# Graph layer with residual norm: every fifth bank of edge counts copied out of PSUM by VectorE

## The chip, the cores and the metric

One NeuronCore of a Trainium2 chip runs the whole kernel. The metric is the device time of one execution in microseconds (us), as the median of several runs. TensorE multiplies matrices into PSUM, VectorE and ScalarE work on vectors and can read PSUM, GpSimd and SyncE serve DMAs here.

## The reference

The graph has N = 6250 nodes of D = 128 features and E = 206250 edges, sorted by their destination:

```
msg = x[src] + edge_attr
agg = segment_sum(msg, dst, N)
h = relu(agg @ W1 + b1) @ W2 + b2
h = (h - mean(h)) * rsqrt(var(h) + 1e-5) * ln_w + ln_b
h = graph_norm(h)
out = layernorm(x + gelu(h) + x)
```

The change touches only how the sums of `x[src]` over the edges of a node are made.

## The kernel before

**Sums of x as a product with counts.** Row `x[src]` is never fetched. The kernel takes 25 chunks of 250 destination nodes. For a chunk it makes `counts[p, q, n]`, how many edges go from source node 128q + p to node n, and then multiplies: 49 tiles q, each as a high and a low part of x (`x_hi`, `x_lo`), so 98 matmuls of 128x250 that add up in one PSUM bank (`count_chunk`, L689 to L695).

**Counts as products of marks.** The 250 nodes of a chunk are 125 pairs. For each pair up to 128 edges lie in 128 partitions, and VectorE writes two tables of ones and zeros, of the source's low seven bits and of its tile and place in the pair (`mark_batch`, L971 to L984, two instructions at L982 for 25 pairs; five batches in a chunk). One matmul of the two tables gives the counts of one pair, 98 columns of PSUM (L672). Five pairs fill a bank of 490 columns, so a chunk has 25 banks, numbered k = 0 to 24. They go round a ring of three PSUM banks (`cps`, `RING = 3`), and ScalarE copies each into `counts` (`copy_chunk`, L514 to L526). TensorE waits for ScalarE's copy of bank k - 3 before it writes bank k (L669), and for all 25 before the 98 matmuls (L689).

**Between the banks.** After banks 2, 8, 14 and 20 TensorE sums half a group of `edge_attr` rows (`sum_half`, L622, a burst of 12 fp32 matmuls that the trace counts as 24) and after the first and third of these turns the sums of the last group (`turn_sums`, L636). After bank 20 it waits for VectorE's keys of the next chunk and turns them (`turn_keys`, L653 to L657), and ScalarE copies the turned keys (`copy_keys`, L495) before its copies of banks 21 to 24.

**VectorE's order** is written by hand. While TensorE does the 98 matmuls, `head` makes batches 0 to 2 of the chunk's marks (slots for three batches, so batch 3 must wait until batch 0 is used up, that is until bank 4 is done). Then `rest` (L1016 to L1028) adds the finished sums (`add_chunk`, L1034), finds rows for the next chunk (`stage_row`), makes batch 3, marks and adds for the edge groups (`mark` L875, `add` L892, `put` L880), makes batch 4, and at last `make_keys` (L949 to L969), a chain of nine short instructions on rows that GpSimd gathered. The next chunk's `head` begins with `stage_tile` (L935).

Ahead of the 25 chunks lies a stage for the index lists and the first edge groups, behind them the two dense layers and the norms. The change leaves both alone.

Of the kernel before, what the change touches and what calls it, by code (L numbers as in the profile page):

```python
# [39 lines left out]
PAIR = 2  # L40
# [4 lines left out]
BATCHES = PAIRS // BATCH  # L45
# [4 lines left out]
BANK = 5  # L50
BANKS = PAIRS // BANK
BPB = BATCH // BANK
CREDIT = BPB + 1
RING = 3
SHIFT = 7
DST_SHIFT = 13
NO_EDGE = (1 << 30) - 1
# [13 lines left out]
def gnn_kernel(nc, x, src, dst, edge_attr, W1, b1, W2, b2, ln_w, ln_b, gn_w, gn_b, gn_ms, out):  # L71
# [37 lines left out]
    with ExitStack() as ctx:  # L109
# [6 lines left out]
        def sem(name):  # L116
            return ctx.enter_context(nc.semaphore(name))
# [97 lines left out]
        eps = [b[:, 0:D] for b in banks[3:5]]  # L215
        turned_sum = [b[:, D:D + SPREAD] for b in banks[3:5]]
        turn_ps, sps = banks[6], banks[7]
        KEY0, LO0 = 0, P
        zps = [banks[u][:, :].rearrange("p (k n) -> p k n", k=HC) for u in range(2)]
        hps = [banks[2], banks[3]]  # L220
# [42 lines left out]
        marks_ready = sem("marks_ready")  # L263
        banks_done = sem("banks_done")
        banks_free = sem("banks_free")
        chunk_summed = sem("chunk_summed")
        chunk_added = sem("chunk_added")
        cover_in = sem("cover_in")
# [49 lines left out]
        g_rest = edge_attr[g_rest0:g_rest0 + G_REST_P * G_TILES, :].rearrange("(p j) d -> p (j d)", j=G_TILES)  # L318
        g_last = edge_attr[g_rest0 + G_REST_P * G_TILES:E, :].rearrange("(a j) d -> a (j d)", a=1)
        dst_tiles = dst[0:ET * SPAN].rearrange("(t e) -> t e", e=SPAN)  # L320

        def column(a):
            return a.rearrange("(p a) -> p a", a=1)
# [78 lines left out]
        @block.gpsimd  # L402
        def _(pool):
            pool.iota(iota_i[:, :], [[1, P]], base=0, channel_multiplier=0)
            pool.iota(prow_i[:, :], [[0, 1]], base=0, channel_multiplier=1)
            pool.iota(pair_i[:, :], [[PAIR * PAIRS, CHUNKS + 1]], base=0, channel_multiplier=PAIR)
            pool.memset(ones_b[:, :], 1.0)
            pool.memset(ones[:, :], 1.0).then_inc(consts_ready, 1)
            half = SEARCH * PAIRS
            for at, to in ((0, half), (half, NPAIR + 7)):  # L410
                pool.iota(pair_row[:, at:to], [[1, to - at]], base=at, channel_multiplier=0,
                          allow_small_or_imprecise_dtypes=True).then_inc(pair_row_ready, 1)
            for s, places in ((halves_free, HALVES), (sums_copied, 3), (sums_turned, 3), (edges_added, 2),
                              (banks_done, CREDIT), (chunk_summed, 1), (chunk_added, 1)):
                pool.sem_inc(s, places)
            pool.wait_ge(turned, TURNS)
            pool.wait_ge(listed_stored, 64)
            pool.memset(agg[:, :], 0.0).then_inc(agg_zeroed, 1)
            pool.wait_ge(below_ready, 2 * SETS)
            pool.iota(listing[:, 0:P * INTER], [[1, P], [0, INTER]], base=0, channel_multiplier=0,  # L420
                      allow_small_or_imprecise_dtypes=True).then_inc(pads_ready, 1)


            with pool.Fori(0, CHUNKS + 1) as c:
                pool.wait_ge(listed_stored, 64)
                pool.wait_ge(tile_staged, c + 1)
                pool.sem_inc(gathers_begun, 1)
                for k in range(2):
                    pool.indirect_dma_start(begins[0:PAIRS, k * P:(k + 1) * P], None, listed_rows,  # L429
                                            bass.IndirectOffsetOnAxis(tile_slot[0:PAIRS, k:k + 1], 0)  # L430
                                            ).then_inc(begins_loaded, 16)
                pool.wait_ge(row_staged, c + 1)
                pool.sem_inc(gathers_begun, 1)
                pool.indirect_dma_start(near[0:PAIRS, :], None, listed_rows,  # L434
                                        bass.IndirectOffsetOnAxis(row_slot[0:PAIRS, 0:1], 0)
                                        ).then_inc(near_loaded, 16)


            pool.wait_ge(mode_ready, 1)
            with pool.If(pool.value_load(flag_i[0:1, 0:1], min_val=0, max_val=1) > 0):  # L440
                with pool.Fori(0, PASSES * G_GROUPS) as n:
                    pool.wait_ge(group_loaded, (n + 1) * 128)
                    pool.sem_inc(gathers_begun, 1)
                    for j in range(G_TILES):
                        pool.indirect_dma_start(g_edges[:, 2 + j // G_HALF, (j % G_HALF) * D:(j % G_HALF + 1) * D], None, x,
                                                bass.IndirectOffsetOnAxis(edge_src[:, j:j + 1], 0)
                                                ).then_inc(group_gathered, 16)

        @block.scalar
        def _(act):  # L450
# [63 lines left out]
            def copy_chunk(c):  # L514
                act.wait_ge(chunk_summed, c + 1)
                for k in range(BANKS):
                    act.wait_ge(banks_done, c * BANKS + (k + 1 + CREDIT))
                    nodes = BANK * PAIR
                    nc.scalar.copy(counts[:, :, k * nodes:(k + 1) * nodes].rearrange("p q (i m) -> p q i m", m=PAIR),  # L519
                                   cps[k % RING][:, 0:nodes * NT].rearrange("p (i q m) -> p q i m", q=NT, m=PAIR)  # L520
                                   ).then_inc(banks_free, 1)
                    if k in SUMS_AT:
                        j = SUMS_AT.index(k)
                        copy_sums(c * GPC + (LEAD * GPC + j), j)
                    if k == KEYS_AT:
                        copy_keys(c + 1)  # L526
# [61 lines left out]
        def _(pe):  # L588
# [74 lines left out]
            def count_chunk(c):  # L663
                for k in range(BANKS):
                    b = k // BPB
                    if k % BPB == 0:
                        pe.wait_ge(marks_ready, c * BATCHES + (b + 1))
                    if k >= RING:
                        pe.wait_ge(banks_free, c * BANKS + (k + 1 - RING))  # L669
                    for i in range(BANK):  # L670
                        n = (k % BPB) * BANK + i
                        last = nc.tensor.matmul(cps[k % RING][:, i * KEYS:(i + 1) * KEYS],  # L672
                                                mark_lo[b % MARKED][:, n // INTER, :, n % INTER],
                                                mark_key[b % MARKED][:, n // INTER, :, n % INTER],
                                                start=(i == 0), stop=(i == BANK - 1),
                                                skip_group_check=True)
                    last.then_inc(banks_done, 1)
                    if k in BURSTS:
                        u = BURSTS.index(k)
                        g = c * GPC + (LEAD * GPC + u // 2)  # L680
                        begin_half(g, u % 2, edge_loaded[u], (c + LEAD) * 16 + 16)
                        sum_half(u, u // 2, u % 2)
                        if u % 2 == 0:
                            turn_sums(g - 1, (u // 2 - 1) % GPC)
                    if k == KEYS_AT:
                        pe.wait_ge(keys_ready, c * 2 + 2)
                        turn_keys(c + 1)

                pe.wait_ge(banks_free, (c + 1) * BANKS)  # L689
                pe.wait_ge(chunk_added, c + 1)  # L690
                for q in range(NT):
                    for part in (x_hi, x_lo):
                        last = nc.tensor.matmul(sps[:, 0:CHUNK], part[:, q, :], counts[:, q, :],  # L693
                                                start=(q == 0 and part is x_hi), stop=(q == NT - 1 and part is x_lo))
                last.then_inc(chunk_summed, 1)  # L695
# [95 lines left out]
        def _(dve):  # L791
# [142 lines left out]
            def stage_tile(c):  # L934
                dve.tensor_copy(tile_slot[0:PAIRS, :], tile_rows[0:PAIRS, bass.ds(c, 1), :].rearrange(  # L935
                    "p a k -> p (a k)")).then_inc(tile_staged, 1)
# [34 lines left out]
            def mark_batch(c, b):  # L971
# [11 lines left out]
                                             of.to_broadcast([P, BLOCKS_B, n, INTER]), ALU.is_equal)  # L983
                last.then_inc(marks_ready, 1)  # L984

            stage_tile(0)
            with dve.Fori(2, LEAD - 3) as r:
                round_groups(r)
# [27 lines left out]
            def rest(c, before, groups):  # L1016
                g = c * GPC + LEAD * GPC
                base = base_of(g + (1 - GPC))
                if before is not None:
                    add_chunk(before, groups)  # L1020
                stage_row(c + 1)
                mark_batch(c, 3)
                mark(g + 1, 0, 1)
                add(g + (1 - GPC), 1, base, c + 1)
                mark(g + 1, 1, 1)
                put(g + 1, 1)
                mark_batch(c, 4)
                make_keys(c + 1)  # L1028

            def add_chunk(c, groups):  # L1030
                dve.wait_ge(chunk_summed, c + 2)
# [220 lines left out]
```

## Time and profile before

| | us |
|---|---|
| median of three runs | 906.94 (905.07 to 907.28) |
| the profiled execution | 911.31 |
| its span, first to last instruction | 909.3 |
| VectorE busy (share of the span) | 678.4 (75%) |
| ScalarE busy | 383.4 (42%) |
| ScalarE copies of counts, 625 | 318.3 |
| TensorE, 2450 matmuls with the counts | 584.1 busy |

TensorE's busy time is that of modelled ends, which overlap; starts are exact. A row of the timeline merges instructions of one line that follow one another. The number in brackets is idle time of the engine ahead of the row, and behind the arrow stands what ended it. In the table of stretches, PEclk is the granted clock: 1.00 is 2.4 GHz and 0.50 is 1.2 GHz.

### The profile page before, as it was taken

To read this page: it belongs to the slowest core of one execution; us is meant where nothing else is said; L and a number is where in the kernel's file an instruction comes from. 1 tells how busy PE (TensorE), PEld (TensorE's weight loads), DVE (VectorE), ACT (ScalarE), POOL (GpSimd) and SP (SyncE) were. 2 spreads that over 40 slices of the span, in tenths; PEclk is the share of its full clock that TensorE was granted. 3 is DMA by queue.
4 is the path that set the end of the run, shared out by engine and by line. 5 is a ranking of instruction groups with operands and counts; after the bars stand their busy time and mean duration, and the time that the engine had idled before them with its cause. 6 is when DMAs were issued, how large, how long until landed. Compare 5 with 4: busy or idle time off the path is not lost.

```text
span 909.3 us, 25887 instructions
## 1 busy us (share of the span) xinstructions
PE 729.4 (80%) x9449; PEld 633.5 (70%) x9449; DVE 678.4 (75%) x1185; ACT 383.4 (42%) x841; POOL 145.4 (16%) x91
## 2 busy tenths in 40 slices
PE   3486569888988888988889988889988889989950
PEld 2464448777877777877777877777877777877830
DVE  5844777877878877878877878877878877844576
ACT  0200034355433555433554433554434554424464
POOL 1210022120221220221120221220221220200000
PEclk9987989899999999999999999999999999999975
DMA  6669973443334443334444334443334444303004
GB/s 173 228 216 361 360 262 99 124 147 115 104 100 121 147 144 116 106 97 125 147 144 114 107 94 128 147 144 112 109 93 130 147 144 113 94 25 141 0 1 141
DMA packets 89477, 123.25 MB, mean 136 GB/s; under 512 B 9029, under 2 KB 85018, under 8 KB 89260
## 3 DMA queue, kind: packets, MB, share of 16 engines
q1 hardware_dynamic: 78992, 112.83, 39.9%
q0 software_dynamic: 6240, 5.08, 2.1%
q10 hardware_dynamic: 4228, 5.12, 1.8%
q8 instruction: 10, 0.16, 0.1%
q14 instruction: 7, 0.05, 0.0%
HBM read 118.91 MB, written 4.03 MB: 135 GB/s over the span
## 4 chain that ended last, share of the span: by engine, by line
PE 48%; DVE 26%; issue 11%; DMA 7%; ACT 5%; DVEq 2%; ACTq 1%; POOL 0%; SPq 0%; POOLq 0%
PE bank L693 33%; DVE pool_m L982 12%; DMA edges<-in_edge_attr_dram 5%; PE bank L622 3%; PE bank L672 3%; ACT counts L519 3%; DVE onehot L875 3%; PE bank L740 3%; PE bank L750 2%; PE bank L656 1%; PE bank L636 1%; DMA agg<-in_dst_dram 1%; DMA begins<-listed,tile_slot 1%; DVE node_f L965 1%; DVE node_f L957 1%
## 5 line engine op out<-in xcount | busy, mean ns | idle before, releaser
L519 ACT CAST counts<-bank 128x490 fp32r<-128x490 f32 x625 | 318.3, 606 | 324.0 <-PE bank L672 324.0
L693 PE MATMUL bank<-counts,x_hi 128*128 128x250 f32 x1225 | 293.5, 284 | 29.6 <-ACT counts L519 29.6
L693 PE MATMUL bank<-counts,x_lo 128*128 128x250 f32 x1225 | 290.6, 281 | 0.0
L982 DVE TENSOR_TENSOR pool_m<-listing,turned_lo 128x3328 bf16<-128x3328 bf16 x125 | 236.7, 1893 | 30.1 <-PE bank L672 26.7
L693 PEld LDWEIGHTS bank<-counts,x_hi 128*128 128x128 f32 x1225 | 234.8, 192 | 33.4 <-ACT counts L519 33.4
L672 PE MATMUL bank<-pool_m 128*128 128x98 bf16 x3125 | 211.2, 210 | 33.0 <-ACT counts L519 22.7
L693 PEld LDWEIGHTS bank<-counts,x_lo 128*128 128x128 f32 x1225 | 235.2, 192 | 0.0
L672 PEld LDWEIGHTS bank<-pool_m 128*128 128x128 bf16 x3125 | 161.9, 99 | 77.6 <-ACT counts L519 75.2
L982 DVE TENSOR_TENSOR pool_m<-listing,turned_key 128x2548 bf16<-128x2548 bf16 x125 | 184.5, 1476 | 0.0
L622 PE MATMUL bank<-edges,onehot 128*32 128x128 f32 x3228 | 126.7, 293 | 30.1 <-DMA edges<-in_edge_attr_dram 23.3
L429 POOL DMA_INDIRECT begins<-listed,tile_slot x52 | 101.9, 1959 | 297.1 <-DVE tile_slot L935 265.2
L622 PEld LDWEIGHTS bank<-edges,onehot 128*32 128x32 f32 x3228 | 88.8, 116 | 46.7 <-issue 20.7
L434 POOL DMA_INDIRECT begins<-listed,row_slot x26 | 33.0, 1270 | 310.6 <-DVE row_slot L946 298.4
L875 DVE TENSOR_TENSOR onehot<-iota_f,dst_cols 128x384 f32<-128x384 f32 x136 | 74.5, 550 | 1.1 <-PE bank L622 0.9
L1034 DVE TENSOR_TENSOR agg<-agg,bank 128x250 f32 (+1 forms) x25 | 10.4, 416 | 75.4 <-PE bank L693 74.6
L489 ACT COPY sums<-bank 128x128 f32<-128x128 f32 x68 | 20.2, 297 | 85.0 <-PE bank L622 85.0
L892 DVE TENSOR_TENSOR agg<-agg,bank 128x128 f32 x68 | 19.0, 280 | 39.4 <-PE bank L636 38.3
L595 PE MATMUL bank<-ones_b,pool_m 128*125 128x1 bf16 x175 | 19.2, 245 | 23.1 <-DVE pool_m L826 23.1
L595 PEld LDWEIGHTS bank<-ones_b,pool_m 128*125 128x125 bf16 x175 | 19.0, 229 | 23.3 <-DVE pool_m L826 23.3
L636 PE MATMUL bank<-place,sums 128*128 128x128 f32 x136 | 34.7, 339 | 0.4 <-ACT sums L489 0.4
L636 PEld LDWEIGHTS bank<-place,sums 128*128 128x128 f32 x136 | 21.2, 197 | 14.9 <-issue 14.0
L546 ACT ACTIVATE onehot<-bank,b1c 128x250 f32<-128x250 f32 x50 | 20.7, 466 | 25.3 <-PE bank L740 25.3
(149 smaller groups left out, 407.9 us busy)
## 6 DMA issues: line engine op xcount, KB each, us to landing
edges<-in_edge_attr_dram SPq DMA_DIRECT2D x134, 768.0 KB, 4.5
out_dram<-pool_m SPq DMA_DIRECT2D x6, 512.0 KB
begins<-listed,tile_slot POOLq DMA_INDIRECT x52, 4.2
agg<-in_dst_dram SPq DMA_DIRECT2D x1, 768.0 KB
agg<-in_src_dram ACTq DMA_DIRECT2D x1, 768.0 KB
listed<-agg ACTq DMA_DIRECT2D x1, 768.0 KB
begins<-listed,row_slot POOLq DMA_INDIRECT x26, 4.3
w<-in_L_gnn_W_dram ACTq DMA_DIRECT2D x2, 128.0 KB, 2.2
```

What stands on the lines that cost most here:

```text
L429: pool.indirect_dma_start(begins[0:PAIRS, k * P:(k + 1) * P], None, listed_rows, bass.IndirectOffsetOnAxis(tile_slot[0:PAIRS, k:k + 1], 0) ...
L434: pool.indirect_dma_start(near[0:PAIRS, :], None, listed_rows, bass.IndirectOffsetOnAxis(row_slot[0:PAIRS, 0:1], 0)).then_inc(near_loaded, 16)
L519: nc.scalar.copy(counts[:, :, k * nodes:(k + 1) * nodes].rearrange("p q (i m) -> p q i m", m=PAIR), cps[k % RING][:, 0:nodes * NT].rearran ...
L546: nc.scalar.activation(hidden[:, u, c, :], zps[u][:, c, 0:CHUNK], ACT.Relu, bias=b1c[:, c:c + 1]).then_inc(hidden_ready, 1)
L595: last = nc.tensor.matmul(turn_ps[0:PAIRS, c:c + 1], below[:, i % BELOW, at:at + PAIRS], ones_b[:, :], start=(c == 0 and i == 0), stop=(i ...
L622: last = nc.tensor.matmul(eps[s][b * WINDOW:(b + 1) * WINDOW, :], oh[:, t, :], edges[:, u, t * D:(t + 1) * D], start=(k == 0 and j == 0), ...
L636: nc.tensor.matmul(turned_sum[s], sums[:, :], place[:, s, :], start=True, stop=True).then_inc(sums_turned, 1)
L672: last = nc.tensor.matmul(cps[k % RING][:, i * KEYS:(i + 1) * KEYS], mark_lo[b % MARKED][:, n // INTER, :, n % INTER], mark_key[b % MARKED ...
L693: last = nc.tensor.matmul(sps[:, 0:CHUNK], part[:, q, :], counts[:, q, :], start=(q == 0 and part is x_hi), stop=(q == NT - 1 and part is ...
L740: last = nc.tensor.matmul(zps[u][:, k, 0:CHUNK], w1[:, k * P:(k + 1) * P], agg[:, bass.ds(c * CHUNK, CHUNK)], start=True, stop=True, skip_ ...
L875: dve.tensor_tensor(oh, window, of.to_broadcast([P, HALF, WINDOW]), ALU.is_equal).then_inc(onehot_ready, 1)
L982: last = dve.tensor_tensor(to[b % MARKED], values[:, :, 0:n, :].to_broadcast([P, BLOCKS_B, n, INTER]), of.to_broadcast([P, BLOCKS_B, n, IN ...
```

## The change

The last bank of each batch (k = 4, 9, 14, 19 and 24) now goes into a PSUM bank of its own (`own_ps`, the unused `banks[5]`), and VectorE copies it (`copy_bank`). The other 20 banks of a chunk keep the ring of three and ScalarE. A new semaphore `own_free` tells TensorE that the bank of its own has been copied. In `rest` the five copies stand between the other steps, and batch 4 moves ahead of `add`, the second `mark` and `put`. The core of the diff:

```diff
+SHARED = BPB - 1
+        own_ps = banks[5]
+        own_free = sem("own_free")
...
 def copy_chunk(c):
     act.wait_ge(chunk_summed, c + 1)
     for k in range(BANKS):
-        act.wait_ge(banks_done, c * BANKS + (k + 1 + CREDIT))
-        nodes = BANK * PAIR
-        nc.scalar.copy(counts[:, :, k * nodes:(k + 1) * nodes].rearrange("p q (i m) -> p q i m", m=PAIR),
-                       cps[k % RING][:, 0:nodes * NT].rearrange("p (i q m) -> p q i m", q=NT, m=PAIR)
-                       ).then_inc(banks_free, 1)
+        if k % BPB < SHARED:
+            act.wait_ge(banks_done, c * BANKS + (k + 1 + CREDIT))
+            nc.scalar.copy(bank_counts(k), in_order(cps[(k - k // BPB) % RING])).then_inc(banks_free, 1)
...
 def count_chunk(c):
-        if k >= RING:
-            pe.wait_ge(banks_free, c * BANKS + (k + 1 - RING))
+        own, turn = k % BPB == SHARED, k - b
+        to = own_ps if own else cps[turn % RING]
+        if own:
+            pe.wait_ge(own_free, c * BATCHES + (b + 1))
+        elif turn >= RING:
+            pe.wait_ge(banks_free, c * (BATCHES * SHARED) + (turn + 1 - RING))
...
-    pe.wait_ge(banks_free, (c + 1) * BANKS)
+    pe.wait_ge(banks_free, (c + 1) * (BATCHES * SHARED))
+    pe.wait_ge(own_free, (c + 1) * BATCHES + 1)
...
+def copy_bank(c, b):
+    dve.wait_ge(banks_done, c * BANKS + ((b + 1) * BPB + CREDIT))
+    dve.tensor_copy(bank_counts(b * BPB + SHARED), in_order(own_ps)).then_inc(own_free, 1)
...
 def rest(c, before, groups):
     stage_row(c + 1)
+    copy_bank(c, 0)
     mark_batch(c, 3)
     mark(g + 1, 0, 1)
+    copy_bank(c, 1)
+    mark_batch(c, 4)
     add(g + (1 - GPC), 1, base, c + 1)
     mark(g + 1, 1, 1)
     put(g + 1, 1)
-    mark_batch(c, 4)
+    copy_bank(c, 2)
     make_keys(c + 1)
+    copy_bank(c, 3)
+    copy_bank(c, 4)
```

The change moves instructions on VectorE and TensorE. First, VectorE in `rest`, from the end of `stage_row` on. Before (`pool_m` holds the marks, `onehot` those of the edge groups):

```order
L946 TENSOR_SCALAR row_slot<-first_i 125x1 [waits prep]
L978 REGISTER_ALU
L982 TENSOR_TENSOR pool_m<-listing,turned_lo 128x3328 [waits banks_done]
L982 TENSOR_TENSOR pool_m<-listing,turned_key 128x2548
L872 ISA
L875 ISA [waits halves_free]
L875 TENSOR_TENSOR onehot<-iota_f,dst_cols 128x384
L887 REGISTER_ALU
L892 ISA [waits chunk_added,edges_added,sums_turned]
L892 TENSOR_TENSOR agg<-agg,bank 128x128
L872 REGISTER_ALU
L875 ISA [waits halves_free]
```

and now, where the row `counts<-bank` is a copy of a bank (49 tiles by 10 nodes):

```order
L959 TENSOR_SCALAR row_slot<-first_i 125x1 [waits prep]
L1000 REGISTER_ALU
L1001 CAST counts<-bank 128x49x10 [waits banks_done]
L995 TENSOR_TENSOR pool_m<-listing,turned_lo 128x3328 [waits banks_done]
L995 TENSOR_TENSOR pool_m<-listing,turned_key 128x2548
L885 ISA
L888 ISA [waits halves_free]
L888 TENSOR_TENSOR onehot<-iota_f,dst_cols 128x384
L1000 REGISTER_ALU
L1001 CAST counts<-bank 128x49x10 [waits banks_done]
L995 TENSOR_TENSOR pool_m<-listing,turned_lo 128x3328 [waits banks_done]
L995 TENSOR_TENSOR pool_m<-listing,turned_key 128x2548
```

The copy of bank 4 stands ahead of batch 3 and the copy of bank 9 ahead of batch 4; the addition to `agg` is gone from between the two batches.

Second, VectorE up to the start of `make_keys` (`lo_i`, `hi_i`, `junk`). Before:

```order
L875 TENSOR_TENSOR onehot<-iota_f,dst_cols 128x384
L880 ISA [waits sums_turned]
L880 TENSOR_SCALAR place<-iota_f,place_row 128x128
L978 REGISTER_ALU
L982 TENSOR_TENSOR pool_m<-listing,turned_lo 128x3328 [waits banks_done]
L982 TENSOR_TENSOR pool_m<-listing,turned_key 128x2548
L950 ISA
L953 TENSOR_SCALAR lo_i<-begins 125x128 [waits near_loaded]
L954 TENSOR_SCALAR hi_i<-begins 125x128
L956 TENSOR_SCALAR junk<-begins 125x128
```

and now:

```order
L888 TENSOR_TENSOR onehot<-iota_f,dst_cols 128x384
L893 ISA [waits sums_turned]
L893 TENSOR_SCALAR place<-iota_f,place_row 128x128
L1000 REGISTER_ALU
L1001 CAST counts<-bank 128x49x10 [waits banks_done]
L963 ISA
L966 TENSOR_SCALAR lo_i<-begins 125x128 [waits near_loaded]
L967 TENSOR_SCALAR hi_i<-begins 125x128
L969 TENSOR_SCALAR junk<-begins 125x128
L943 REGISTER_ALU
L970 REGISTER_ALU [waits prep]
```

Batch 4 no longer stands right ahead of the keys; the copy of bank 14 does. The copies of banks 19 and 24 come behind the keys.

Third, TensorE at the end of a chunk's counts, banks 23 and 24, with the numbers of the PSUM banks. Before:

```order
L669 REGISTER_ALU
L672 MATMUL bank2<-pool_m 128x98 [waits banks_free]
L672 MATMUL bank2<-pool_m 128x98 x4
L669 REGISTER_ALU
L672 MATMUL bank0<-pool_m 128x98 [waits banks_free]
L672 MATMUL bank0<-pool_m 128x98 x4
L689 ISA
L693 MATMUL bank7<-counts,x_hi 128x250 [waits chunk_added,banks_free]
```

and now:

```order
L681 REGISTER_ALU
L684 MATMUL bank1<-pool_m 128x98 [waits banks_free]
L684 MATMUL bank1<-pool_m 128x98 x4
L684 MATMUL bank5<-pool_m 128x98 [waits own_free]
L684 MATMUL bank5<-pool_m 128x98 x4
L701 ISA
L702 ISA [waits banks_free]
L706 MATMUL bank7<-counts,x_hi 128x250 [waits chunk_added,own_free]
```

Bank 24 goes to PSUM bank 5 and waits for VectorE's copy of bank 19; the first of the 98 matmuls waits for ScalarE's copies and for VectorE's.

## Rows read from the trace of the kernel before

**Rows 1.** The page's first part: busy us, share of the span, instructions.

```profile
PE 729.4 (80%) x9449; PEld 633.5 (70%) x9449; DVE 678.4 (75%) x1185; ACT 383.4 (42%) x841; POOL 145.4 (16%) x91
```

**Rows 2.** Timeline of VectorE, addition of each chunk's sums (start us, us, instruction, idle before).

```profile
154.48 0.42 DVE L1034 TENSOR_TENSOR agg<-agg,bank 128x250 f32 x1 [2.90 <-PE bank L693]
...
184.57 0.42 DVE L1034 TENSOR_TENSOR agg<-agg,bank 128x250 f32 x1 [5.72 <-PE bank L693]
...
213.38 0.42 DVE L1034 TENSOR_TENSOR agg<-agg,bank 128x250 f32 x1 [4.43 <-PE bank L693]
...
240.70 0.41 DVE L1034 TENSOR_TENSOR agg<-agg,bank 128x250 f32 x1 [2.94 <-PE bank L693]
...
786.87 0.42 DVE L1034 TENSOR_TENSOR agg<-agg,bank 128x250 f32 x1 [2.90 <-PE bank L693]
```

**Rows 3.** Timeline of TensorE, one steady chunk, from its first bank to its sums.

```profile
404.18 0.87 PE L672 MATMUL bank<-pool_m 128*128 128x98 bf16 x15
...
404.98 0.86 PE L622 MATMUL bank<-edges,onehot 128*32 128x128 f32 x24
...
406.10 0.87 PE L672 MATMUL bank<-pool_m 128*128 128x98 bf16 x15
...
415.09 0.86 PE L622 MATMUL bank<-edges,onehot 128*32 128x128 f32 x24
...
416.92 0.33 PE L656 MATMUL bank<-ident,lo_f 125*128 125x125 f32 x1 [0.97 <-DVE junk L967]
...
417.19 0.86 PE L672 MATMUL bank<-pool_m 128*128 128x98 bf16 x15
...
419.95 0.39 PE L693 MATMUL bank<-counts,x_hi 128*128 128x250 f32 x1 [1.19 <-ACT counts L519]
```

**Rows 4.** Timeline of VectorE in the same chunk, from batch 3 to the next chunk.

```profile
406.76 1.93 DVE L982 TENSOR_TENSOR pool_m<-listing,turned_lo 128x3328 bf16<-128x3328 bf16 x1 [0.89 <-PE bank L672]
...
410.02 0.54 DVE L875 TENSOR_TENSOR onehot<-iota_f,dst_cols 128x384 f32<-128x384 f32 x1
...
414.55 0.21 DVE L953 TENSOR_SCALAR lo_i<-begins 125x128 int32<-125x128 int32 x1
...
416.57 0.28 DVE L967 TENSOR_SCALAR_CACHE_REDUCE junk<-junk 125x128 f32<-125x128 f32 x1
...
416.78 0.08 DVE L967 DVE_READ_ACCUMULATOR junk<-junk  x1
...
417.43 0.17 DVE L935 COPY tile_slot<-tile_rows 125x2 int32 x1 [0.56 <-DVE junk L967]
```

**Rows 5.** Timeline of ScalarE, the end of the same chunk.

```profile
417.39 0.27 ACT L499 CAST turned_lo<-bank 128x125 bf16<-128x125 f32 x1 [1.27 <-PE bank L656]
...
417.70 1.55 ACT L519 CAST counts<-bank 128x490 fp32r<-128x490 f32 x3
...
419.25 0.66 ACT L519 CAST counts<-bank 128x490 fp32r<-128x490 f32 x1
```

**Rows 6.** Timeline of VectorE late in the kernel, and one group by form.

```profile
878.45 0.67 DVE L1174 SCALAR_TENSOR_TENSOR pool_m<-pool_m,bank 128x512 f32 x1
...
879.03 1.64 DVE L1179 BATCH_NORM_STATS2 pool_m<-pool_m  x8
...
L862 DVE CAST dst_cols<-bank 128x408 bf16<-128x408 f32 x4 | 7.6, 2197 | 0.0
```

**Rows 7.** Stretches of TensorE: from:to us, length, PE busy (count), PEclk, DMA share, GB/s.

```profile
164.90:169.20 4.30, 2.47 (x50) 0.99 0.80 258
169.20:176.00 6.80, 6.16 (x29) 0.50 0.19 61
195.60:199.90 4.30, 1.86 (x35) 1.00 0.78 255
199.90:203.30 3.40, 3.38 (x16) 0.50 0.09 28
415.00:419.30 4.30, 2.48 (x50) 1.00 0.78 258
```

More of the change, by code:

```diff
@@ L320, in gnn_kernel, with bank_counts, in_order @@
         dst_tiles = dst[0:ET * SPAN].rearrange("(t e) -> t e", e=SPAN)
+        def bank_counts(k):
+            nodes = BANK * PAIR
+            return counts[:, :, k * nodes:(k + 1) * nodes].rearrange("p q (i m) -> p q i m", m=PAIR)
+        def in_order(bank):
+            return bank[:, 0:BANK * KEYS].rearrange("p (i q m) -> p q i m", q=NT, m=PAIR)
         def column(a):
@@ L413, in _ @@
             for s, places in ((halves_free, HALVES), (sums_copied, 3), (sums_turned, 3), (edges_added, 2),
-                              (banks_done, CREDIT), (chunk_summed, 1), (chunk_added, 1)):
+                              (banks_done, CREDIT), (chunk_summed, 1), (chunk_added, 1), (own_free, 1)):
                 pool.sem_inc(s, places)
@@ L667, in count_chunk @@
                         pe.wait_ge(marks_ready, c * BATCHES + (b + 1))
-                    if k >= RING:
-                        pe.wait_ge(banks_free, c * BANKS + (k + 1 - RING))
+                    own, turn = k % BPB == SHARED, k - b
[4 more added lines that the diff above has]
+                        pe.wait_ge(banks_free, c * (BATCHES * SHARED) + (turn + 1 - RING))
                     for i in range(BANK):
                         n = (k % BPB) * BANK + i
-                        last = nc.tensor.matmul(cps[k % RING][:, i * KEYS:(i + 1) * KEYS],
+                        last = nc.tensor.matmul(to[:, i * KEYS:(i + 1) * KEYS],
                                                 mark_lo[b % MARKED][:, n // INTER, :, n % INTER],
```

## The prediction

> **What bounds the kernel now.** The page's first part comes first: TensorE is busy 80% of the span, VectorE 75%, ScalarE 42% [rows 1]. No engine is full, so the order of waits inside a chunk has to be read. The timeline of VectorE gives the length of a chunk from one addition of sums to the next: (786.87 - 240.70) / 20 = 27.31 us in the steady part [rows 2]. The timeline of TensorE parts such a chunk in two: 25 banks of counts from 404.18 to 419.95, that is 15.77 us, and the 98 matmuls, the other 11.54 us [rows 3]. The matmuls follow one another without a gap, so the change can only act in the 15.77 us.
>
> The reader should see there that TensorE doesn't set the pace. It writes three banks in 0.80 us (404.18 to 404.98), a bank in 0.27, and it sits idle for 0.97 us before it turns the keys at 416.92 and for 1.19 us before the matmuls at 419.95 [rows 3]. The first wait ends with VectorE, the second with ScalarE. VectorE's timeline shows why the first is there: it waits 0.89 us for bank 4, starts batch 3 at 406.76, and from there works without a pause to the end of the keys at 416.78 + 0.08 = 416.86 [rows 4]. **This chain of 10.1 us on VectorE, not the copies on ScalarE, sets when the counts can end.** From the keys to the matmuls it is ScalarE: the turned keys from 417.39, banks 21 to 23 from 417.70 to 419.25, then bank 24 until 419.91 [rows 5], 0.04 us before the first matmul.
>
> **The price of a copy on VectorE.** No copy of this shape is in the trace. The nearest row is the addition late in the kernel that reads 512 columns of fp32 from PSUM: 0.67 us long, and the next instruction starts 0.58 us after it [rows 6]. For 490 columns I take 0.58 x 490 / 512 = 0.56 us of VectorE's time, with its end 0.65 us after its start. A lower bound is half of it, 0.28, if a copy with one source ran at twice the rate. An upper bound is the conversion of `dst_cols`, also out of PSUM: 2197 ns for 408 elements [rows 6], 5.4 ns each, so 2.6 us for 490. That row writes single two-byte values 48 bytes apart; the new copies write ten neighbouring words at a time, so I stay with 0.56.
> The Trainium skill (Vector Engine (DVE) Microarchitecture Reference, section Measured stream behaviour on trn2) states full rate for runs of at least two adjacent words, which the copies have on both sides; by it the upper bound falls away. No row here shows it for this shape.
>
> **Part by part, in a steady chunk.**
> - Removed from ScalarE: five copies. Four of them end nothing that is late. Taking away that of bank 24 lets ScalarE end with bank 23 at 419.25 in place of 419.91: 0.66 us gained at the end of the chain [rows 5].
> - Added to VectorE ahead of the keys: the copies of banks 4, 9 and 14. The first can't use the 0.89 us wait, since it waits for the same bank 4 as batch 3 behind it. All three lie in the unbroken chain: 3 x 0.56 = 1.68 us. Keys at 418.54 in place of 416.86.
> - Batch 4 ahead of the addition, the second mark and the `place`: the same instructions in another order, nothing for the keys.
> - Added behind the keys: the copies of banks 19 and 24. Bank 24 is written 4 x 0.27 = 1.07 us after the turn at 417.19, so at 418.26; with a 0.13 us hand-over and 0.65 us its copy ends at 419.04 on the old clock, before ScalarE's 419.25. Hidden, by 0.2 us.
> - VectorE's next chunk: `stage_tile`, at 417.43 before [rows 4], must now wait for the copy of bank 24, and starts about 3.8 us later, the tables some 3.4 us later (0.36 us of the old gap was a wait for the keys). The matmuls start 1.02 us later. VectorE's wait for them was 2.94 us [rows 2], so about 0.5 us of cover is left. If it were gone, batch 3 would be late next.
> - TensorE's new waits: bank 14 needs the copy of bank 9, which starts at 406.76 + 0.56 + 3.26 + 0.54 = 411.1 and ends at 411.8. After it come a burst and a turn (404.98 to 406.10, 1.12 us) and banks 15 to 18, until about 414.2. Bank 19 needs the copy of bank 14, which starts at 414.55 + 1.12 = 415.7 and ends at 416.3 [rows 3, 4]. Behind that wait stand bank 20 and a burst, 1.3 us, done by 417.7; the keys come at 418.5. Hidden behind the keys, but TensorE is now empty for about 2.1 us at one place and 0.9 at another.
>
> Sum without the clock: 1.68 - 0.66 = 1.02 us a chunk, 25.5 us for 25 chunks.
>
> **The clock.** In two chunks of the kernel before, the granted clock fell to 0.50 at the end of the counts: from 169.2 to 176.0 and from 199.9 to 203.3 [rows 7]. These chunks took 184.57 - 154.48 = 30.09 and 213.38 - 184.57 = 28.81 us, 2.78 and 1.50 more than the steady 27.31 [rows 2]. In the 4.3 us ahead of the falls TensorE was busy 2.47 and 1.86 us; in the steady chunk the stretch like the first has 2.48 and the clock stays up [rows 7]. So the kernel before stands close to the edge. The change makes the stretch emptier: in the 4.3 us from 414.2 to the keys at 418.5 TensorE has 1.3 us of work. I therefore expect a fall in nearly every chunk. Its price is between 1.50 and 2.78, mean 2.14; I add 0.2, since the turn of the keys (0.27 us), now at the lower clock as well, lies on the path: 2.3 us. For 24 chunks, the first one left out, 55.2 us.
> The Trainium skill (TensorE: Matmul & The Clock Gate, section HAM oscillation) puts the danger in single long gaps of TensorE; by that rule the gaps here would be too short and the term nothing, 932.4 us in all. The falls of the two chunks came with gaps of about 1 us, as the steady chunk's 0.97 and 1.19 [rows 3], so the trace speaks against it.
>
> **The forecast.** The profiled execution took 911.31 us, 4.37 above the median of 906.94. The two falls in it (2.78 + 1.50 = 4.28) explain nearly all of that, and I put every chunk's clock into its own term: 911.31 - 4.28 + 25.5 + 55.2 = 987.7, so **988 us**.
>
> **The rivals.**
> - *The clock stays up*, or falls as seldom as before: for it, the steady chunk, which has such gaps and keeps it; against it, the emptier stretch. 906.94 + 25.5 = 932.4 us. If it falls in half of the chunks, 932.4 + 12 x 2.3 = 960.
> - *The copies come cheap and the end of the chain is what counts* (faster): ScalarE's last copy ends 0.66 us earlier in each chunk, and the copies on VectorE find room in its waits. Then 906.94 - 25 x 0.66 = 890.4 us. It decides where the three copies together cost less than 0.66 us, 0.22 each, in the chain. Against it: even the lower bound of 0.28 is above that, and there is no pause in the chain [rows 4]. At that lower bound the chunk loses 0.84 - 0.66 = 0.18 us, 911 us without falls.
> - *The copies are slow because of their strides*: with 2.6 us each the keys come 7.8 us later, 7.1 us a chunk, and the time passes 1080.
> - *The change does not do what it says*, in that ScalarE stays the last in a chunk: that is so in my sum too, and there its gain is only the 0.66.
>
> **How the numbers follow.** A measurement here tells 0.3% from no change. Falls in nearly every chunk: 0.62, from 907 + 25.5 + 24 x 1.50 = 968.5 to 907 + 25.5 + 24 x (2.78 + 0.2) = 1004. Falls in about half: 0.12. None or few: 0.17. Slower copies, over 1005: 0.03. These are slower, 0.94. Break-even near 0.22 us a copy: 0.03 for no change. The cheap copies: 0.03 for faster. The range goes from 930, which takes in the case without falls, to 1005.
>
> **What would show it.** On VectorE's timeline, three copies of about 0.65 us between batch 3 and the keys, and keys some 1.7 us later after bank 4. On TensorE's, a wait of about 2 us ahead of bank 19 that ends with VectorE, and a chunk length near 30.6 us (28.3 without falls). In the stretches, a granted clock of 0.50 at the start of the 98 matmuls in most chunks. The forecast is wrong if the copies start to end in well under 0.3 us, if VectorE waits between batch 3 and the keys, or if the clock reads 1.00 throughout.

## The result: 991.15 us, 1.0924 times the time before

| | before | after |
|---|---|---|
| median of four runs each, us | 907.11 (905.07 to 909.91) | 991.15 (989.94 to 992.18) |
| ratio, 95% interval | | 1.0924 (1.089 to 1.0957) |
| the profiled execution, its span | 911.31, 909.3 | 989.94, 987.9 |

The kernel lost 84.0 us; 988 was predicted. The size and the sign came out, but the trace shows that two steps of the working did not happen as told. The profile page of the kernel after has this in its first part, its line of the granted clock, and its row for the new copies (busy us, mean ns, idle time before them):

```profile
PE 756.1 (77%) x9449; PEld 671.8 (68%) x9449; DVE 751.3 (76%) x1310; ACT 328.4 (33%) x716; POOL 139.9 (14%) x91
...
PEclk9976778988889888899888998889988899889975
...
L1001 DVE CAST counts<-bank 128x490 fp32r<-128x490 f32 x125 | 83.0, 664 | 95.2 <-PE bank L684 95.2
```

Against [rows 1] VectorE gained 125 instructions and 73 us of busy time, ScalarE lost 55. The clock is down all along the 25 chunks, not in two of them.

VectorE's timeline of the kernel after, additions of two chunks (start us, us, instruction, idle before):

```profile
525.30 0.42 DVE L1056 TENSOR_TENSOR agg<-agg,bank 128x250 f32 x1 [1.31 <-PE bank L706]
...
556.02 0.41 DVE L1056 TENSOR_TENSOR agg<-agg,bank 128x250 f32 x1 [1.30 <-PE bank L706]
```

A chunk takes 556.02 - 525.30 = 30.72 us, where it took 27.31 [rows 2]: 3.41 more. VectorE's wait for the matmuls shrank from 2.90 to 1.31 and did not vanish. Between those rows, VectorE's timeline of the same chunk:

```profile
527.48 0.67 DVE L1001 CAST counts<-bank 128x490 fp32r<-128x490 f32 x1 [0.89 <-PE bank L684]
528.06 1.88 DVE L995 TENSOR_TENSOR pool_m<-listing,turned_lo 128x3328 bf16<-128x3328 bf16 x1
...
531.73 0.66 DVE L1001 CAST counts<-bank 128x490 fp32r<-128x490 f32 x1
532.30 1.88 DVE L995 TENSOR_TENSOR pool_m<-listing,turned_lo 128x3328 bf16<-128x3328 bf16 x1
...
535.50 0.28 DVE L905 TENSOR_TENSOR agg<-agg,bank 128x128 f32 x1
...
536.36 0.66 DVE L1001 CAST counts<-bank 128x490 fp32r<-128x490 f32 x1
536.94 0.21 DVE L966 TENSOR_SCALAR lo_i<-begins 125x128 int32<-125x128 int32 x1
...
539.17 0.08 DVE L980 DVE_READ_ACCUMULATOR junk<-junk  x1
540.17 0.67 DVE L1001 CAST counts<-bank 128x490 fp32r<-128x490 f32 x1 [0.92 <-PE bank L684]
542.94 0.67 DVE L1001 CAST counts<-bank 128x490 fp32r<-128x490 f32 x1 [2.10 <-PE bank L684]
```

The copy is 0.66 us long and the next instruction starts 0.57 or 0.58 after it. From bank 4 to the keys VectorE still works without a pause: 527.48 to 539.25 is 11.77 us, 1.67 more than the 10.10 of [rows 4]. But the keys are not what TensorE waits for. Its timeline in the same chunk:

```profile
524.89 0.87 PE L684 MATMUL bank<-pool_m 128*128 128x98 bf16 x15
...
532.44 0.40 PE L684 MATMUL bank<-pool_m 128*128 128x98 bf16 x5 [1.25 <-DVE counts L1001]
535.83 1.51 PE L630 MATMUL bank<-edges,onehot 128*32 128x128 f32 x24 [2.99 <-DVE agg L905]
...
537.86 2.69 PE L684 MATMUL bank<-pool_m 128*128 128x98 bf16 x30
540.48 1.12 PE L630 MATMUL bank<-edges,onehot 128*32 128x128 f32 x24
541.52 0.33 PE L664 MATMUL bank<-ident,lo_f 125*128 125x125 f32 x1
...
544.09 0.36 PE L706 MATMUL bank<-counts,x_hi 128*128 128x250 f32 x1 [1.19 <-ACT counts L529]
```

Bank 14 waits 1.25 us for the copy of bank 9, and the burst behind it 2.99 us for `add` on VectorE (L905, 535.50 to 535.78). The burst of the first half of an edge group waits for that `add` (in `begin_half`: `if k == 0: pe.wait_ge(edges_added, g + 1)`). Rows of the kernel before, from VectorE's and from TensorE's timeline, show the same pair with time to spare:

```profile
410.49 0.27 DVE L892 TENSOR_TENSOR agg<-agg,bank 128x128 f32 x1
...
411.61 0.86 PE L622 MATMUL bank<-edges,onehot 128*32 128x128 f32 x24
```

There `add` was over at 410.76 and the burst began at 411.61; now batch 4 and two copies stand ahead of `add`. Behind the wait the burst takes 1.51 us in place of 0.86: the clock is down. So TensorE comes to the turn of the keys at 541.52, 2.27 us after they lay ready. The stretches of TensorE (from:to us, length, PE busy and count, PEclk, DMA share, GB/s) give the clock:

```profile
529.00:534.30 5.30, 2.39 (x51) 0.99 0.81 260
534.40:541.20 6.80, 5.37 (x72) 0.51 0.39 116
541.30:543.80 2.50, 1.60 (x34) 1.00 0.36 46
544.20:555.60 11.40, 11.40 (x98) 1.00 0.18 61
```

0.51 is the level of 1.2 GHz. It lies on the second half of the counts and not on the 98 matmuls, which run at 1.00; stretches of the other chunks show the same fall in each of the 24 chunks after the first. The list of waits (engine and line, what for, us in total, times, longest) has the wait for `add` in all 25, 3.0 us each, and the waits for copies on VectorE:

```profile
PE bank L630 <- DVE agg L905: 74.5, 25, 3.0
...
PE bank L684 <- DVE counts L1001: 37.8, 26, 5.9
```

**The 3.41 us of a chunk.** From the first bank to the first of the 98 matmuls it is now 544.09 - 524.89 = 19.20 us, against 15.77 [rows 3], 3.43 more. That is +1.67 of VectorE's chain, +2.21 of TensorE's lateness (2.27 in place of 0.06), and -0.46 at the end (turn of the keys to first matmul 2.57, before 3.03): 3.42.

### The profile page after: what moved, and what is told of

Same layout as the page of the kernel before. It is cut to its first block, busy times and chain, and to the rows that moved or that the text cites. A ratio compares the mean times of both kernels' runs of the same rounds, so it can differ in the third digit from the quotient of the medians.

```text
span 987.9 us, 25736 instructions
## 1 busy us (share of the span) xinstructions
PE 756.1 (77%) x9449; PEld 671.8 (68%) x9449; DVE 751.3 (76%) x1310; ACT 328.4 (33%) x716; POOL 139.9 (14%) x91
## 4 chain that ended last, share of the span: by engine, by line
PE 58%; DVE 18%; issue 11%; DMA 6%; ACT 3%; DVEq 2%; ACTq 1%; POOL 0%; SPq 0%; POOLq 0%
PE bank L706 30%; DVE pool_m L995 10%; PE bank L630 10%; PE bank L684 9%; DMA edges<-in_edge_attr_dram 4%; PE bank L644 3%; ACT counts L529 2%; PE bank L763 2%; PE bank L753 2%; DVE counts L1001 2%; DVE onehot L888 1%; DMA agg<-in_dst_dram 1%; PE bank L664 1%; DMA begins<-listed,tile_slot 1%; PE bank L603 1%
## 5 line engine op out<-in xcount | busy, mean ns | idle before, releaser
L529 ACT CAST counts<-bank 128x490 fp32r<-128x490 f32 x500 | 258.9, 590 | 471.3 <-PE bank L684 467.5
L706 PE MATMUL bank<-counts,x_hi 128*128 128x250 f32 x1225 | 288.9, 281 | 29.8 <-ACT counts L529 29.8
L706 PE MATMUL bank<-counts,x_lo 128*128 128x250 f32 x1225 | 287.0, 279 | 0.0
L684 PEld LDWEIGHTS bank<-pool_m 128*128 128x128 bf16 x3125 | 184.5, 109 | 68.7 <-DVE counts L1001 41.9
L630 PE MATMUL bank<-edges,onehot 128*32 128x128 f32 x3228 | 151.3, 334 | 92.9 <-DVE agg L905 74.5
L630 PEld LDWEIGHTS bank<-edges,onehot 128*32 128x32 f32 x3228 | 105.2, 133 | 115.8 <-DVE agg L905 78.3
L439 POOL DMA_INDIRECT begins<-listed,tile_slot x52 | 95.2, 1831 | 425.2 <-DVE tile_slot L948 387.9
L1001 DVE CAST counts<-bank 128x490 fp32r<-128x490 f32 x125 | 83.0, 664 | 95.2 <-PE bank L684 95.2
L905 DVE TENSOR_TENSOR agg<-agg,bank 128x128 f32 x68 | 19.1, 281 | 38.0 <-PE bank L644 37.0
L644 PE MATMUL bank<-place,sums 128*128 128x128 f32 x136 | 43.4, 411 | 0.4 <-ACT sums L499 0.4
L644 PEld LDWEIGHTS bank<-place,sums 128*128 128x128 f32 x136 | 27.0, 248 | 20.0 <-issue 19.2
```

The costliest lines, as they stand in the source:

```text
L529: nc.scalar.copy(bank_counts(k), in_order(cps[(k - k // BPB) % RING])).then_inc(banks_free, 1)
L630: last = nc.tensor.matmul(eps[s][b * WINDOW:(b + 1) * WINDOW, :], oh[:, t, :], edges[:, u, t * D:(t + 1) * D], start=(k == 0 and j == 0), ...
L644: nc.tensor.matmul(turned_sum[s], sums[:, :], place[:, s, :], start=True, stop=True).then_inc(sums_turned, 1)
L684: last = nc.tensor.matmul(to[:, i * KEYS:(i + 1) * KEYS], mark_lo[b % MARKED][:, n // INTER, :, n % INTER], mark_key[b % MARKED][:, n // I ...
L1001: dve.tensor_copy(bank_counts(b * BPB + SHARED), in_order(own_ps)).then_inc(own_free, 1)
```

## The experiments

My theory after the result: half of the loss is the path, half the clock, and the clock falls because the burst waits for `add`. The rival: the copies alone do it, and the order is innocent. `hold(n)` in the diffs below adds n matmuls of 256 columns of `x_hi` into PSUM columns that nothing reads; they do no work of the kernel and only keep TensorE busy. Ratios are to the kernel before on the same chip; the experiments ran on several chips, on which the kernel before took 907.5 to 909.0 us. Chunk lengths leave out the last chunk, whose sums are added after the loop.

**Clock held up in the changed kernel (`e1_hold`).**

```diff
+                    if k == 14:
+                        hold(22)
                     if k in BURSTS:
```

> The changed kernel with 22 extra matmuls of 256 columns after bank 14 of each chunk, about 2.6 us of TensorE work into unused columns of a PSUM bank, placed where TensorE now waits 3.0 us for VectorE's addition. Theory clock: the fall of the granted clock costs about 1.9 us of the 30.72 us of a chunk; with TensorE kept at work the clock reads 1.00 through the chunk, a chunk takes about 28.8 us and the kernel about 945 us. Rival, the waits alone cost the time and the clock only shows them: a chunk stays at 30.7 us or gets longer by the extra work, 990 us or more.

Measured: 947.63 us, ratio 1.0426 (1.0381 to 1.047). TensorE's timeline and two additions of VectorE's:

```profile
510.14 2.88 PE L673 MATMUL bank<-x_hi 128*128 128x256 f32 x22
513.31 0.86 PE L630 MATMUL bank<-edges,onehot 128*32 128x128 f32 x24 [0.29 <-DVE agg L912]
...
517.10 0.33 PE L664 MATMUL bank<-ident,lo_f 125*128 125x125 f32 x1
```

```profile
502.78 0.42 DVE L1063 TENSOR_TENSOR agg<-agg,bank 128x250 f32 x1 [1.32 <-PE bank L713]
...
531.56 0.41 DVE L1063 TENSOR_TENSOR agg<-agg,bank 128x250 f32 x1 [1.28 <-PE bank L713]
```

and the stretch of TensorE over this chunk:

```profile
502.80:531.50 28.70, 25.51 (x350) 1.00 0.39 116
```

The burst takes 0.86 again, the clock reads 1.00, and the chunk takes 28.78 us (28.79 in most). With nothing useful added, 991.15 - 947.63 = 43.5 us of the 84.0 go: they were the clock's. The rest, 28.79 - 27.31 = 1.48 us a chunk, is the path.

**The order alone (`e2_order_alone`),** on the kernel before, no copies moved.

```diff
                 mark(g + 1, 0, 1)
+                mark_batch(c, 4)
                 add(g + (1 - GPC), 1, base, c + 1)
                 mark(g + 1, 1, 1)
                 put(g + 1, 1)
-                mark_batch(c, 4)
                 make_keys(c + 1)
```

> The kernel before, all copies on ScalarE, with one edit: batch 4 of the marks ahead of the addition, the second mark and the place. Theory order: the burst after bank 14 waits for the addition, some 2.5 to 3 us; without falls of the clock a chunk takes about 28.8 us, with a fall in each about 30.7 us and the kernel about 985 us. Rival, the copies on VectorE alone make the loss and the order costs nothing, as the prediction had it: 907 us.

Measured: 1025.83 us, ratio 1.1276 (1.1203 to 1.135), slower than either theory said. Chunks take 29.5 to 34.1 us. TensorE's timeline and stretches:

```profile
675.87 1.51 PE L622 MATMUL bank<-edges,onehot 128*32 128x128 f32 x24 [2.34 <-DVE agg L892]
```

```profile
674.00:686.00 12.00, 7.84 (x103) 0.68 0.46 143
686.00:699.00 13.00, 13.00 (x89) 0.77 0.10 39
```

The wait for `add` is there without a single copy on VectorE, so the order makes it. In the chunk shown, of 34.10 us, the clock falls twice, in the counts and again in the 98 matmuls; so it is in 12 of the 24 chunks, and in the other 12 it falls once, at either place.

**The copies alone (`e3_copies_alone`):** the changed kernel with `add`, the mark and `put` back ahead of batch 4.

```diff
                 copy_bank(c, 1)
-                mark_batch(c, 4)
                 add(g + (1 - GPC), 1, base, c + 1)
                 mark(g + 1, 1, 1)
                 put(g + 1, 1)
+                mark_batch(c, 4)
                 copy_bank(c, 2)
```

> The changed kernel with the addition, the second mark and the place put back ahead of batch 4; the five copies stay on VectorE. Theory copies, as the prediction had it: keys 1.7 us later, TensorE waits some 2 us for the copy of bank 14 ahead of bank 19, the clock falls in nearly every chunk, 30.6 us a chunk, 985 to 990 us; without falls 28.4 us and 932 us. Theory order alone: no wait of TensorE for the addition, so close to the kernel before, 907 to 915 us.

Measured: 988.61 us, ratio 1.0865 (1.0812 to 1.0917), chunks 30.71. TensorE's timeline and stretches:

```profile
535.05 0.64 PE L684 MATMUL bank<-pool_m 128*128 128x98 bf16 x10 [1.71 <-DVE counts L1001]
...
537.28 0.47 PE L664 MATMUL bank<-ident,lo_f 125*128 125x125 f32 x1 [0.80 <-DVE junk L980]
```

```profile
533.40:537.50 4.10, 1.65 (x35) 0.97 0.49 177
537.60:544.40 6.80, 6.04 (x42) 0.52 0.40 121
```

This is the kernel that the prediction described: bank 19 waits for the copy of bank 14, the keys are late, and the fall begins with the turn of the keys and lasts into the 98 matmuls. Either part alone gives chunks of 30.7 us or more (nearly all of them), so the two do not add up: 30.72 together. The rival is right that the copies alone make a loss of this size, and wrong that the order is innocent. My own theory holds for the place of the fall in the changed kernel, not for the size of the loss.

**The copies alone, clock held up (`e7_copies_hold`),** with `hold(16)` after bank 18 and `hold(6)` ahead of the keys.

```diff
+                    if k == 18:
+                        hold(16)
...
                     if k == KEYS_AT:
+                        hold(6)
                         pe.wait_ge(keys_ready, c * 2 + 2)
```

> The kernel of the run with the copies alone (addition ahead of batch 4) with extra matmuls in its two idle places: 16 after bank 18 (1.9 us) and 6 ahead of the keys (0.7 us). If the prediction's two terms are right each by itself, the clock reads 1.00, the chunk is the prediction's sum without the clock, 27.3 + 1.0 = 28.3 to 28.5 us, and the kernel 932 to 938 us; the rest of the 988.6 us of the run with the copies alone is the clock. If the copies cost more than 1.0 us on the path, a chunk stays above 29.5 us and the kernel above 960.

Measured: 942.33 us, ratio 1.0361 (1.0318 to 1.0404); 19 of the chunks take 28.51 to 28.53 us at a granted clock of 1.00; four take 29.6, and in these the clock still falls once. TensorE's timeline:

```profile
513.86 0.28 PE L664 MATMUL bank<-ident,lo_f 125*128 125x125 f32 x1
...
516.42 0.36 PE L714 MATMUL bank<-counts,x_hi 128*128 128x250 f32 x1 [1.25 <-ACT counts L529]
```

Turn to matmuls is 2.56 us, 0.47 less than before, and 1.67 - 0.47 = 1.20 is the 28.52 - 27.31 = 1.21 measured. The clock's share of the copies is 30.71 - 28.52 = 2.2 us a chunk.

**The order alone, clock held up (`e12_order_hold`):** `e2_order_alone` with `hold(18)` after bank 14.

```diff
+                    if k == 14:
+                        hold(18)
                     if k in BURSTS:
```

> The kernel with the order alone (1025.8 us, chunks of 30.7 to 34.1 us), with 18 extra matmuls (2.1 us) into the unused PSUM bank after bank 14, where TensorE waits 2.3 us for the addition. If the order costs its wait and the rest is the clock: 28.8 us a chunk, 945 us, some chunks with a fall at the end of the counts, up to 960. If the order lengthens the path by itself to over 30 us: 980 us and more.

Measured: 997.09 us, ratio 1.0974 (1.0935 to 1.1014): a miss. TensorE's timeline at the end of the counts, and ScalarE's:

```profile
512.66 0.33 PE L656 MATMUL bank<-ident,lo_f 125*128 125x125 f32 x1
...
516.71 0.39 PE L700 MATMUL bank<-counts,x_hi 128*128 128x250 f32 x1 [2.21 <-ACT counts L519]
```

```profile
513.45 0.60 ACT L519 CAST counts<-bank 128x490 fp32r<-128x490 f32 x1
514.97 1.05 ACT L519 CAST counts<-bank 128x490 fp32r<-128x490 f32 x2 [0.93 <-PE bank L677]
```

The fall behind bank 14 is gone (the burst takes 0.86), but from turn to matmuls it is now 4.05 us, against 3.03 [rows 3]: ScalarE stands idle 0.93 us between its copies of the last banks. Chunks take 28.7 to 32.5 us, and the one shown, of 29.70, is one of only two before the last in which the clock stays at 1.00. In the other 21 it falls at the end of the counts or the start of the 98 matmuls. TensorE's stretches, first of such a chunk (30.75 us), then of the chunk of 28.67 us, whose clock stays up and whose turn of the keys comes at 483.99:

```profile
542.40:545.90 3.50, 1.49 (x26) 0.99 0.69 213
545.90:549.20 3.30, 3.21 (x15) 0.50 0.35 117
...
484.00:487.00 3.00, 1.53 (x26) 1.00 0.71 197
487.00:498.50 11.50, 11.48 (x98) 1.00 0.15 53
```

In the chunk of 28.67 us ScalarE has no such pause: the matmuls come 3.03 us after the turn, as before, and the turn 1.41 us after the keys in place of 0.06. So the order's own price on the path is 28.67 - 27.31 = 1.36 us, close to the 28.8 expected. The rest of what the order alone costs is a second fall of the clock, at the end of the counts, which the changed kernel has in no chunk after the first, and pauses of ScalarE, 0.2 to 0.9 us, in the chunks with that fall and in the one shown. The profile puts these pauses down to TensorE, though in the chunk shown its banks were written by then; what ScalarE waits for, and why the fall is there in one kernel and not in the other, stay open.

**Does a busy TensorE by itself gain anything? (`e9_before_hold`):** the kernel before with `hold(7)` in its wait for the keys.

> Control for the extra matmuls: the kernel before with 7 of them (0.85 us) in the 0.97 us in which TensorE waits for the keys. They do no useful work and lie in a wait, so if they act through the clock alone a chunk stays at 27.3 us and the two early falls go: 903 to 907 us. If the extra matmuls by themselves changed the path, the chunk length would differ from 27.3 us.

Measured: 907.63 us beside 907.58, ratio 0.9992 (0.9976 to 1.0008). Its chunks take 27.3 us. The extra matmuls are worth nothing where the clock is up already.

**Was ScalarE's ring the bound? (`e4_ring4`):** the kernel before with the unused PSUM bank as a fourth place in the ring.

```diff
-RING = 3
+RING = 4
...
-        cps = banks[0:RING]
+        cps = banks[0:3] + [banks[5]]
```

> The kernel before with the fifth PSUM bank as a fourth place in ScalarE's ring; no work moves. TensorE stops waiting for ScalarE between banks, but the keys from VectorE still end the counts: 27.3 us a chunk and 907 us if the path alone counts. If the clock decides, TensorE gets done with bank 20 sooner and is idle longer ahead of the keys, the clock falls more often, and the time rises to between 910 and 945 us.

Measured: 908.71 us, ratio 0.9989 (0.9961 to 1.0017). It was not: the chain on VectorE sets the end of the counts with three places or four.

**Only the copy that is on the path (`e5_only24`):** bank 24 alone goes to its own PSUM bank, and VectorE copies it behind the keys; the order is that of before.

```diff
+OWN = BANKS - 1
...
                 mark_batch(c, 4)
                 make_keys(c + 1)
+                copy_bank(c)
```

> The kernel before with only bank 24 in a PSUM bank of its own and copied by VectorE, behind the keys. The gain of 0.66 us at the end of the chain should come without the copies ahead of the keys: 26.65 us a chunk where the clock stays up, 890 us. If the clock falls again in several chunks, since a chunk no longer has the length that kept it up, 895 to 907 us. If the copy on VectorE ends as late as ScalarE's did, no change, 907.

Measured: 905.48 us, ratio 0.9962 (0.994 to 0.9984). 14 chunks take 26.66 us, 0.65 less than before, as the term of 0.66 says; nine take 28.1 to 28.2, since the clock falls in them. 25 x 0.65 = 16 us gained, 9 x 1.5 = 14 given back.

**The same, clock held up (`e6_only24_hold`),** with `hold(7)` ahead of the keys.

> As the run with bank 24 alone, with 7 extra matmuls (0.85 us) while TensorE waits for the keys. Theory clock: no falls, 26.65 us a chunk, 890 us, whatever the run without them gives. If the clock doesn't matter there, the same time as the run without them.

Measured: 891.70 us, ratio 0.9794 (0.975 to 0.9838); every chunk takes 26.63. What `e5_only24` had given back to the clock is there.

**A shorter chain too (`e8_only24_marks`, `e11_marks_alone`):** both marks of the second edge group move from `rest` to the end of `head`, where VectorE waits for the 98 matmuls; the first on `e5_only24`, the second on the kernel before.

```diff
                 mark_batch(c, 2)
+                mark(g + 1, 0, 1)
+                mark(g + 1, 1, 1)
...
                 mark_batch(c, 3)
-                mark(g + 1, 0, 1)
                 add(g + (1 - GPC), 1, base, c + 1)
-                mark(g + 1, 1, 1)
                 put(g + 1, 1)
```

> As the run with bank 24 alone, with the two marks of the chunk's second edge group moved from the chain ahead of the keys into the time in which VectorE waits for the 98 matmuls. If the chain from batch 3 to the keys sets the end of the counts, as the prediction read it, the keys come 0.94 us earlier and TensorE's idle time of 0.97 us ahead of them goes: 25.7 us a chunk, no falls, 866 to 870 us. If ScalarE's copies are what TensorE waits for by then, 26.2 to 26.6 us and 880 to 890 us.

> The kernel before, all copies on ScalarE, with only the two marks of the second edge group moved into VectorE's wait for the matmuls. It parts the gain of the fastest version: 0.94 us a chunk from the chain, 26.4 us a chunk, 884 us; the 0.66 us of bank 24 would then be the rest down to 867.7. If ScalarE then ends the counts whatever the keys do, 27.0 us a chunk and 900 us.

Measured: **867.68 us, ratio 0.9535 (0.9495 to 0.9574)**, faster than both kernels, with no extra matmuls; the marks alone 889.93, ratio 0.9798 (0.976 to 0.9836), where 884 was expected: the clock falls in seven chunks, which take 27.9 us. Rows of `e8_only24_marks`, VectorE's marks and additions, TensorE's turn, and a stretch:

```profile
512.92 1.02 DVE L888 TENSOR_TENSOR onehot<-iota_f,dst_cols 128x384 f32<-128x384 f32 x2
514.03 0.42 DVE L1052 TENSOR_TENSOR agg<-agg,bank 128x250 f32 x1
...
539.69 0.41 DVE L1052 TENSOR_TENSOR agg<-agg,bank 128x250 f32 x1
```

```profile
525.48 0.33 PE L664 MATMUL bank<-ident,lo_f 125*128 125x125 f32 x1
```

```profile
513.70:525.40 11.70, 10.67 (x207) 1.00 0.62 179
```

The two marks (1.02 us) fill the wait that stood ahead of the addition, and the keys meet a TensorE that has just finished its burst: no idle time ahead of the turn, where it was 0.97 [rows 3]. The chunk is 25.66 us, and the clock stays at 1.00.

## Why the prediction was right, and where it was not

- **What bounds the kernel: right.** A fourth ring place gained nothing, and the two marks taken off VectorE's chain, where they stood for 0.94 us, gained 0.98 a chunk (`e11_marks_alone`, 26.33 in the chunks without a fall).
- **The price of a copy: right.** 0.66 us long, next start after 0.57 or 0.58, forecast 0.65 and 0.56; three of them 1.67, forecast 1.68.
- **The end of the chain: too large.** "0.66 us gained" is 0.65 in `e5_only24`, but 0.46 in the changed kernel and 0.47 in `e7_copies_hold`. In `e5_only24` and in the changed kernel alike ScalarE's last copy ends 2.3 us after the turn; the 0.2 lies between that end and the first matmul (0.05 and 0.24 us), and its cause stays open.
- **"Batch 4 ahead of the addition ...: nothing for the keys": this is the step that failed.** It is true of the keys and beside the point. `add` has a second waiter, the burst after bank 14. In the trace of before that wait is not seen, because `add` ends 0.85 us early; the move puts it a batch (3.20 us) and two copies (1.15) later. The 2.1 us of idle TensorE that I set ahead of bank 19 came as 2.99 ahead of this burst (and 1.25 ahead of bank 14). The time hardly shows it: with the order left as it was, a chunk takes 30.71 us (`e3_copies_alone`), with it 30.72.
- **The clock: it fell as forecast, at another place.** It fell in every chunk (forecast: nearly every), but in the second half of the counts. The price is 30.72 - 28.79 = 1.93 us, forecast 2.3; in `e3_copies_alone`, where the fall lies where I had put it, 2.2. The reason given for it is weaker than it reads. [rows 7] sets 1.86 us busy ahead of the second fall beside 2.48 in the steady chunk, but these are not the same part of a chunk; the part of the steady chunk that answers to the second has 1.86 too, at a clock of 1.00:

```profile
415.62:419.92 4.30, 1.86 (x35) 1.00 0.78 257
```

So these stretches of the kernel before do not tell the chunks with a fall from those without. What the runs show is that filling the waits takes most falls away (`e1_hold`, `e6_only24_hold`, `e7_copies_hold`); in which chunks the clock falls otherwise stays open. The Trainium skill (TensorE: Matmul & The Clock Gate, section HAM oscillation) puts the danger in single long waits; `e3_copies_alone`, where the clock falls with waits of 1.71 and 0.80 us, shows that shorter ones can be enough.
- **The path: too small.** 1.48 a chunk, forecast 1.02. Of the 0.46 between, 0.2 is the smaller gain at the end, and the other 0.27 is the order (28.79 - 28.52): even with the clock held up, TensorE comes to the turn 0.37 us after the keys (517.10 against 516.73).
- **VectorE's next chunk: mis-summed, without harm.** By the prediction's own terms the copy of bank 24 starts at 418.26 + 0.13 + 1.68 = 420.07 and frees VectorE 0.56 later, so `stage_tile` starts at 420.63, 3.2 us after 417.43 and not 3.8. Of the wait for the matmuls 1.31 us were left, not 0.5.
- **The sum came out by two errors that cancel:** 1.48 + 1.93 = 3.41 against 1.02 + 2.3 = 3.32. For the kernel without the new order the two terms are nearer, 1.21 and 2.2. That the order added to the path what its earlier fall saved was luck, so 988 is close to 991.15 partly for a wrong reason.
- **The rivals.** The copies were neither cheap nor slowed by strides. Had the clock stayed up, it would have been 947.6 (`e1_hold`); that rival's 932.4 was 15 us low, 25 x 0.46 = 11.5 of them by the path.

## What to carry to other kernels

Before a step is moved past another on one engine, list every engine that waits for its semaphore, those that did not have to wait in the trace before as well, and give each its slack (here 0.85 us, against a move of over 4). Where the clock of TensorE is close to falling, price what empties TensorE apart from what lengthens the path: here each cost about half, and a version that shortened the path by 16 us gained 2.4 until the clock was held. Of five copies, move the one that stands on the path: it was worth 0.65 us a chunk, and three of the others cost 1.67.

## What the runs showed of the hardware

- An fp32 copy of 490 columns out of PSUM by VectorE, that reads runs of two words and writes runs of ten, took 664 ns on average, and the addition that reads 512 columns 670 ns [rows 6]: no price for the strides is seen.
- The granted clock fell after waits of 1.7 and 0.8 us as after one of 2.99, and matmuls that nothing reads, put into waits, were worth 43.5 us in the changed kernel and 13.8 in `e5_only24`, and cost nothing where the clock was up (`e9_before_hold`). They are no sure means: `e12_order_hold` lost one fall by them and kept another in 21 chunks.
- The fall does not follow from the chunk alone: in the kernel before it came in two chunks and not in the others, with TensorE 1.86 us busy in the same 4.30 us of a chunk with and without it.
- A run of equal chunks can hold the fall in each of them (30.3 to 30.7 us in the kernel after), or in some (`e5_only24`, 9 of 24).
